# Self-attention followed by a frequency-split convolution: the running maxima spread over other steps, the low parts of kept blocks moved to the end of a step, four of them to GpSimd

## The chip, the cores and the metric

The kernel runs on one core of a Trainium2 chip. Its engines work side by side, each through its own list of instructions, and meet only at semaphores: TensorE (PE; PEld is its weight load), VectorE (DVE), ScalarE (ACT), GpSimd (POOL) and SyncE (SP), which issues all of this kernel's transfers. The metric is the time of one execution on the device, in microseconds (us).

## The reference

Four images of 256 channels and 64 x 64 pixels, all in float32. Layer 0 is self-attention over the 4096 pixels, layer 1 a convolution of two frequency bands:

```python
# layer 0
q = einsum('qc,bcn->bqn', Wq, xf); k = einsum('qc,bcn->bqn', Wk, xf); v = einsum('vc,bcn->bvn', Wv, xf)
attn = softmax(einsum('bqn,bqm->bnm', q, k) * 32 ** -0.5, axis=-1)      # 4096 x 4096 per image
x = gamma[0] * einsum('oc,bchw->bohw', Wo, einsum('bvm,bnm->bvn', v, attn)) + x
# layer 1, on patches of 8 x 8 pixels
low = p.reshape(B * nP, C, 4, 2, 4, 2).mean(axis=(3, 5)); high = p - up2_nearest(low)
low = prelu(bn(einsum('oc,nchw->nohw', mag_w, low) + mag_b))
hs = concatenate([high, roll(high, 1, axis=2)], axis=1)
high = prelu(bn(einsum('oc,nchw->nohw', phase_w, hs) + phase_b))[:, :C]
out = up2_nearest(low) + high
```

## The kernel before

**Turns.** The 4096 query pixels of an image are cut into 8 chunks of 512. One pass over all keys for one chunk is a turn `g`; there are 32 of them. Inside turn `g` three things run interleaved: the attention of chunk `g`, the maxima that the softmax of chunk `g + 1` needs, and the convolution of a chunk whose attention is done. Turns 0 to 23 follow the plan `FULL` (they also project the keys and values of the next image), turns 24 to 30 the plan `LAST`, turn 31 `FINAL`. In turns 0 to 15 (called scan turns here) VectorE also scans a chunk of x of a later image for its largest magnitude (step `SCAN` = 12, L906).

**Steps.** A turn has 32 steps, listed in `UNITS`; each takes one unit, which is 12 matmuls of 128x257 or 128x256 into the four banks `O`. A direct unit `("d", i)` multiplies probabilities that are computed from a product `S` of keys and queries (L597): ScalarE writes them as f16 (`ph`, L765) and as f32 (`p`, L768), VectorE subtracts the two and gives the low part `pl` (L1049). A kept unit `("k", k)` takes scores that were kept in `saved` when their maximum was taken a turn earlier: ScalarE makes `pq` high and the f32 value (L776, L777), VectorE the low part (L1054), and a DMA transposes both into `pt` (L377), because they lie the other way round. Steps 0 to 5 are d0 to d5; then kept and direct units alternate (k0 in step 6, d6 in step 7, k1 in step 8, up to d15 in step 25); steps 26 to 31 are k10 to k15. So in the middle of a turn an even step is a kept unit and an odd step a direct one.

**Tasks.** `Plan` gives each step its tasks. The tasks of a plan take the two banks `M0` and `M1` in turn, so task n can't start on TensorE before task n - 2 has been read out. `("max", j, m)` is one matmul (L526) of 128 queries against 512 keys; VectorE reduces it to a maximum, for m below 4 alone (L949), for m from 4 on it writes the scores to `saved` as well (L953). There are 32 of them in a turn. `steps_with_maxima` gives one to each step from `first` on, and two to the steps in `DOUBLE`. `("negmax",)` turns the maxima into a row for the next turn's products; `("y", h)`, `("low", o)` and `("high", o)` belong to the convolution, `("kq",)` and `("u", h)` to the projections.

**Order on an engine.** The order is written out in the program. In VectorE's step t come first the low part `pl` of the unit of step t + 1, then the low part `pq` of the kept unit of step t + 4, then the scan, then the maxima of step t. SyncE transposes the kept units in their order (`turn_slot`, L374 to L378); between them, at fixed places, it issues the other transfers: after k2 the load `xb` (L422), after k3 the load `xr` that the scan reads (L432), each behind whatever its predecessors wait for. GpSimd splits the frequencies (L301 to L314), makes the low parts of x and of the convolution's input (L1178, L322 to L325), and adds up the output (L1214 to L1223).

Of the kernel before, what the change touches and what calls it, by code (L numbers as in the profile page):

```python
# [29 lines left out]
CH = 512  # L30
# [15 lines left out]

DOUBLE = (7, 8, 10, 12, 14, 16, 18)

ND, NK = MT // 2, MT // 2
# [7 lines left out]
AT = {unit: t for t, unit in enumerate(UNITS)}  # L57
EXP_AHEAD, LOW_AHEAD = 5, 4


def slots_at(t, ahead):

    return [k for k in range(NK) if AT["k", k] - ahead == t]


MAXIMA = [(j, m) for j in range(SUB) for m in range(NCH) if m not in TURNED] + [(j, m) for m in TURNED for j in range(SUB)]


def slot_of(j, m):

    return (m - TURNED[0]) * SUB + j
# [17 lines left out]

def steps_with_maxima(steps, first=4, doubled=DOUBLE):  # L90

    left = list(MAXIMA)
    t = first
    while left:
        for _ in range(2 if t in doubled else 1):
            j, m = left.pop(0)
            assert m not in TURNED or t >= AT["k", slot_of(j, m)] - LOW_AHEAD
            steps.setdefault(t, []).append(("max", j, m))
        t += 1
    steps[t + 1] = [("negmax",)]  # L100
    return steps
# [6 lines left out]
LAST = Plan(steps_with_maxima({4: [("y", 0)], 5: [("y", 1)], 19: [("low", 0, 1)], 21: [("high", 0)], 23: [("high", 1)]},  # L108
                              first=3, doubled=(6, 8, 10, 12, 14, 16, 18)),
            before=(FULL, ALL - NCH))  # L110
# [8 lines left out]
def attention_conv(nc, x, wqk, wv, wo, phase_w, mag_w, params, gamma, alpha, out, q_dram):  # L119
# [7 lines left out]
    with ctx:  # L127
# [103 lines left out]
        s_filled, probs_ready, lo_ready = sem("s_filled"), sem("probs_ready"), sem("lo_ready")  # L231
        slot_probs, slot_low, turn_seen = sem("slot_probs"), sem("slot_low"), sem("turn_seen")
        turned = [sem(f"turned{i}") for i in range(RING)]
        d_weighed, k_weighed, nmax_done, bias_ready = sem("d_weighed"), sem("k_weighed"), sem("nmax_done"), sem("bias_ready")
# [96 lines left out]
        def _(sp):  # L331
# [40 lines left out]
            def turn_slot(g, k):  # L372

                sp.wait_ge(slot_low, NK * g + k + 1)  # L374
                sp.wait_ge(k_weighed, NK * g + k + 1)
# [326 lines left out]
        def _(act):  # L702
# [107 lines left out]
            def turn(g, parity, c, plan, scans):  # L810
# [8 lines left out]
                for t, (unit, i) in enumerate(UNITS):  # L819
                    if t > 0 and unit == "d" and i + LEAD < ND:  # L820
                        probabilities(g, i + LEAD)
                    for k in slots_at(t, EXP_AHEAD):
                        slot_probabilities(g, k)
                    for n, task in plan.numbered.get(t, []):
# [39 lines left out]
        def _(dve):  # L864
# [206 lines left out]
            def take(n, task, g, parity, c, plan):  # L1071
# [12 lines left out]
                elif kind in ("y", "max", "negmax"):  # L1084
# [3 lines left out]
                    elif kind == "max":  # L1088
                        if task[2] in TURNED:
                            dve.wait_ge(slot_low, NK * g + slot_of(*task[1:]) + 1)  # L1090
                            saved_max(bank, task[1], task[2], free)
                        else:
                            partial_max(bank, task[1], task[2], free)
# [11 lines left out]
            def turn(g, parity, c, plan, scans):  # L1105
# [6 lines left out]
                for t in range(MT):  # L1112
                    if t == MT - 2 and plan is LAST:
                        finish_chunk(g)
                    if t + 1 < MT and UNITS[t + 1][0] == "d":
                        low_probabilities(g, UNITS[t + 1][1])
                    for k in slots_at(t, LOW_AHEAD):
                        slot_low_probabilities(g, k)
                    if t == (0 if plan is FULL else 1):
# [6 lines left out]
                    for n, task in plan.numbered.get(t, []):  # L1126
                        take(n, task, g, parity, c, plan)
                    if t == NEGATIVE:
                        negative_parts(plan, g)
# [36 lines left out]
        def _(pool):  # L1166
# [45 lines left out]
            def add_up(g):  # L1212
# [11 lines left out]
                ins.then_inc(out_ready, 1)  # L1224

            def turn(g, parity, c, plan, scans):
                split_frequencies(pool, nc.gpsimd, plan, g)
                if plan is FULL:
                    low_x(0, xbl, xb, xbh, g + EVEN_FIRST + 1)
                low_conv_in(pool, nc.gpsimd, g)  # L1230
                add_up(g)

# [33 lines left out]
```

## Time and profile before

| what | value |
|---|---|
| time, median of 3 runs | 2338.88 us (2338.19 to 2339.94) |
| profiled execution, its own time | 2340.89 us |
| span of the profiled execution | 2338.8 us |
| mean granted TensorE clock | 0.985 |

The span runs from the first to the last instruction; the execution's own time is 2.1 us longer. The turn whose rows are shown below most is turn 12, a scan turn, from 955.8 to 1026.5 us. Its step 9 begins at 976.92, step 13 at 984.81, step 15 at 989.95 and step 17 at 993.55: a direct step begins with its product `S` (L597).

### The profile page before, as it was taken

How to read it: one execution, taken by the hardware profiler on the slowest of the kernel's cores; microseconds unless marked ns; L12 is line 12 of the kernel's file. 1: busy time of each engine (PE TensorE's matmuls, PEld its weight loads, DVE VectorE, ACT ScalarE, POOL GpSimd, SP SyncE). 2: the span in 40 equal slices, each digit the busy share in tenths (PEclk: the TensorE clock that was granted, in tenths of full speed). 3: DMA queues.
4: the chain of work that ended last, by engine and by line, in shares of the span. 5: the costliest groups of instructions: out<-in, count | busy, mean ns of one | idle time of the engine just before them, and what ended most of it. 6: DMA issues, size and time to landing. Idle time of an engine off the chain costs nothing.

```text
span 2338.8 us, 48151 instructions
## 1 busy us (share of the span) xinstructions
PE 2211.5 (95%) x16373; PEld 1768.0 (76%) x16373; DVE 1745.7 (75%) x3388; ACT 1435.3 (61%) x2547; POOL 664.4 (28%) x891
## 2 busy tenths in 40 slices
PE   5799999999989999999998999999999999999997
PEld 4577778777777777777776877777777777777786
DVE  6777787777867777877777777778777777777764
ACT  3456666657656566666575666666666667666664
POOL 3232332232321323322323223223222322333231
PEclk8899999999999999999999999999999999999998
DMA  4255444354654444443565434544446443444443
GB/s 162 62 101 111 103 99 110 72 110 105 146 126 78 103 110 105 99 107 72 112 148 122 99 79 83 110 93 101 99 100 137 87 93 80 81 89 86 84 87 67
DMA packets 596617, 235.02 MB, mean 100 GB/s; under 512 B 547072, under 2 KB 548352, under 8 KB 596576
## 3 DMA queue, kind: packets, MB, share of 16 engines
q1 hardware_dynamic: 596576, 234.51, 46.2%
q8 instruction: 22, 0.36, 0.1%
q14 instruction: 19, 0.16, 0.0%
HBM read 67.67 MB, written 32.53 MB: 43 GB/s over the span
## 4 chain that ended last, share of the span: by engine, by line
PE 74%; ACT 8%; issue 8%; DVE 7%; POOL 1%; DMA 0%; DVEq 0%; SPq 0%; ACTq 0%; POOLq 0%
PE M L489 13%; PE M L526 9%; PE O L651 8%; PE O L653 8%; PE O L652 8%; PE O L638 8%; PE O L640 7%; PE O L639 7%; PE S L597 4%; DVE pmax L949 3%; ACT pq L776 2%; ACT saved L777 2%; ACT p L768 2%; PE M L507 1%; DVE pl L1049 1%
## 5 line engine op out<-in xcount | busy, mean ns | idle before, releaser
L765 ACT ACTIVATE ph<-S 128x512 f16<-128x512 f32 x512 | 308.0, 602 | 540.0 <-PE S L597 537.2
L638 PE MATMUL O<-uh,ph 128*128 128x257 f16 x2048 | 568.7, 278 | 4.4 <-DVE pl L1049 4.0
L651 PE MATMUL O<-uh,pt 128*128 128x257 f16 x2048 | 568.0, 277 | 0.1
L953 DVE TENSOR_SCALAR_CACHE_REDUCE saved<-M 128x512 f32<-128x512 f32 x512 | 346.6, 688 | 292.5 <-PE M L526 287.0
L640 PE MATMUL O<-uh,pl 128*128 128x257 f16 x2048 | 561.9, 274 | 0.0
L639 PE MATMUL O<-ul,ph 128*128 128x256 f16 x2048 | 560.4, 274 | 0.0
L653 PE MATMUL O<-uh,pt 128*128 128x257 f16 x2048 | 558.9, 273 | 0.0
L652 PE MATMUL O<-ul,pt 128*128 128x256 f16 x2048 | 555.6, 271 | 0.0
L526 PE MATMUL M<-kst,qst 96*128 (+1 forms) x1024 | 424.2, 450 | 53.0 <-DVE pmax L949 33.4
L1054 DVE TENSOR_TENSOR pq<-saved,pq 128x512 f16<-128x512 f32 x512 | 379.4, 741 | 86.2 <-ACT saved L777 80.4
L1049 DVE TENSOR_TENSOR pl<-p,ph 128x512 f16<-128x512 f32 x512 | 375.0, 736 | 54.7 <-ACT p L768 53.2
L776 ACT ACTIVATE pq<-saved,nbias 128x512 f16<-128x512 f32 x512 | 369.0, 721 | 0.0
L777 ACT ACTIVATE saved<-saved,nbias 128x512 f32<-128x512 f32 x512 | 368.0, 719 | 0.0
L949 DVE TENSOR_REDUCE pmax<-M 128x1 f32<-128x512 f32 (+1 forms) x512 | 336.5, 683 | 19.6 <-PE M L526 19.4
L768 ACT ACTIVATE p<-S 128x512 f32<-128x512 f32 x512 | 307.6, 601 | 0.0
L638 PEld LDWEIGHTS O<-uh,ph 128*128 128x128 f16 x2048 | 200.4, 98 | 120.2 <-issue 63.5
L651 PEld LDWEIGHTS O<-uh,pt 128*128 128x128 f16 x2048 | 198.8, 97 | 105.2 <-issue 74.3
L526 PEld LDWEIGHTS M<-kst,qst 96*128 96x128 f32 x1024 | 179.5, 191 | 110.9 <-DVE pmax L949 56.3
L1214 POOL TENSOR_TENSOR zlow<-zlow,zlneg 128x256 f32<-128x256 f32 x32 | 35.4, 1106 | 791.0 <-DVE zneg L1069 791.0
L597 PE MATMUL S<-qcur,kst 128*128 128x512 f32 x512 | 237.2, 473 | 18.2 <-ACT p L768 15.8
L640 PEld LDWEIGHTS O<-uh,pl 128*128 128x128 f16 x2048 | 201.2, 98 | 25.7
L653 PEld LDWEIGHTS O<-uh,pt 128*128 128x128 f16 x2048 | 197.7, 97 | 29.1
(161 smaller groups left out, 2864.9 us busy)
## 6 DMA issues: line engine op xcount, KB each, us to landing
xr<-in_x SPq DMA_DIRECT2D x53, 512.0 KB, 3.7
out_y<-z SPq DMA_DIRECT2D x33, 512.0 KB, 3.0
xb<-in_x SPq DMA_DIRECT2D x25, 512.0 KB, 3.9
pt<-pq SPq DMA_TRANSPOSE x512, 3.1
qraw<-q_scratch SPq DMA_DIRECT2D x99, 64.0 KB, 2.0
uh_scratch<-uh_next SPq DMA_DIRECT2D x24, 257.0 KB, 3.1
uh<-uh_scratch SPq DMA_DIRECT2D x24, 257.0 KB, 3.3
ul_scratch<-ul_next SPq DMA_DIRECT2D x24, 256.0 KB, 3.1
```

The lines of the kernel that those rows point to most:

```text
L526: return nc.tensor.matmul(bank[:, :], qst[0:96, j * 128:(j + 1) * 128], kst[0:96, keys_at], start=True, stop=True)
L638: nc.tensor.matmul(O[j][:, 0:UW], ph[:, i % 4, q], uh[:, i, :], start=(i == 0), stop=False)
L639: nc.tensor.matmul(O[j][:, 0:C], ph[:, i % 4, q], ul[:, i, :], start=False, stop=False)
L640: ins = nc.tensor.matmul(O[j][:, 0:UW], pl[:, i % 4, q], uh[:, i, :], start=False, stop=False)
L651: nc.tensor.matmul(O[j][:, 0:UW], pt[:, k % RING, i, :], uh[:, t, :], start=False, stop=False)
L652: nc.tensor.matmul(O[j][:, 0:C], pt[:, k % RING, i, :], ul[:, t, :], start=False, stop=False)
L653: ins = nc.tensor.matmul(O[j][:, 0:UW], pt[:, k % RING, SUB + i, :], uh[:, t, :], start=False, stop=(ends and i == SUB - 1))
L776: nc.scalar.activation(pq[:, k % RING, 0, :], saved[:, k, :], ACT.Exp, scale=SCALE, bias=bias)
L777: nc.scalar.activation(saved[:, k, :], saved[:, k, :], ACT.Exp, scale=SCALE, bias=bias).then_inc(slot_probs, 1)
L949: nc.vector.tensor_reduce(pmax[:, j, ds(m, 1)], bank[:, :], AX.X, ALU.max).then_inc(free, 1)
L1049: nc.vector.tensor_tensor(pl[:, i % 4, :], p32[:, i % 2, :], ph[:, i % 4, :], ALU.subtract).then_inc(lo_ready, 1)
L1054: nc.vector.tensor_tensor(pq[:, k % RING, 1, :], saved[:, k, :], pq[:, k % RING, 0, :], ALU.subtract).then_inc(slot_low, 1)
```

## The change

It has three parts. The maxima begin in step 3 (before: 4 under `FULL`, 3 under `LAST`), the doubled steps are 8, 10, 15, 17, 25 (before: 7, 8, 10, 12, 14, 16, 18), under `LAST` 8, 10, 12, 15, 17, 26, and the `negmax` task comes in the step right behind the last maximum. The low part of a kept unit moves on VectorE from the head of step AT - 4 to the end of step AT - 3 for k0 to k9, behind the maxima of that step, and for k10 to k15 to the end of step AT - 4. And the low parts of k9 to k12 are made by GpSimd, in two halves of 256 columns each, counted by a semaphore of their own.

```diff
-DOUBLE = (7, 8, 10, 12, 14, 16, 18)
+DOUBLE = (8, 10, 15, 17, 25)
...
-EXP_AHEAD, LOW_AHEAD = 5, 4
...
+POOLED = (9, 10, 11, 12)
+EXP_AT = [AT["k", k] - 5 for k in range(NK)]
+LOW_AT = [AT["k", k] - (3 if k < ND - RISE else 4) for k in range(NK)]
...
+def low_count(g, k):
+
+    if k in POOLED:
+        return len(POOLED) * g + POOLED.index(k) + 1
+    return (NK - len(POOLED)) * g + k - sum(p < k for p in POOLED) + 1
...
-def steps_with_maxima(steps, first=4, doubled=DOUBLE):
+def steps_with_maxima(steps, first=3, doubled=DOUBLE):
...
-    steps[t + 1] = [("negmax",)]
+    steps[t] = [("negmax",)]
...
-                              first=3, doubled=(6, 8, 10, 12, 14, 16, 18)),
+                              doubled=(8, 10, 12, 15, 17, 26)),
...
             def turn_slot(g, k):
 
-                sp.wait_ge(slot_low, NK * g + k + 1)
+                sp.wait_ge(pooled_low if k in POOLED else slot_low, low_count(g, k))
+                sp.sem_inc(turn_seen, 1)
                 sp.wait_ge(k_weighed, NK * g + k + 1)
...
-                    for k in slots_at(t, LOW_AHEAD):
-                        slot_low_probabilities(g, k)
...
                     for n, task in plan.numbered.get(t, []):
                         take(n, task, g, parity, c, plan)
+                    for k in range(NK):
+                        if LOW_AT[k] == t and k not in POOLED:
+                            slot_low_probabilities(g, k)
...
+            def pooled_probabilities(g, k):
+
+                pool.wait_ge(slot_probs, NK * g + k + 1)
+                for n in (slice(0, CH // 2), slice(CH // 2, CH)):
+                    ins = nc.gpsimd.tensor_tensor(pq[:, k % RING, 1, n], saved[:, k, n], pq[:, k % RING, 0, n], ALU.subtract)
+                ins.then_inc(pooled_low, 1)
+
...
                 low_conv_in(pool, nc.gpsimd, g)
+                for k in POOLED:
+                    pooled_probabilities(g, k)
                 add_up(g)
```

VectorE, steps 12 and 13 of a scan turn, before. `pl` and `pq` are the low parts of a direct and a kept unit, `amax<-xr` is the scan, each `pmax<-M` a maximum:

```order
L1049 TENSOR_TENSOR pl<-p32,ph 128x512
L1054 TENSOR_TENSOR pq<-saved,pq 128x512
L1124 REGISTER_ALU
L906 ISA
L906 TENSOR_REDUCE amax<-xr 128x1
L1085 REGISTER_ALU
L949 TENSOR_REDUCE pmax<-M0 128x1
L949 TENSOR_REDUCE pmax<-M1 128x1
L1085 REGISTER_ALU
L949 TENSOR_REDUCE pmax<-M0 128x1
```

The same two steps of the changed kernel:

```order
L1056 TENSOR_TENSOR pl<-p32,ph 128x512
L1130 REGISTER_ALU
L913 ISA
L913 TENSOR_REDUCE amax<-xr 128x1
L1092 REGISTER_ALU
L956 TENSOR_REDUCE pmax<-M0 128x1
L956 TENSOR_REDUCE pmax<-M1 128x1
L1061 TENSOR_TENSOR pq<-saved,pq 128x512
```

Between `pl` and the end of step 13 stood `pq`, the scan and three maxima; now the scan and two maxima stand there, and a `pq` (k5, the same unit) behind them.

VectorE, steps 16 and 17, before; `saved,pmax<-M` is a maximum whose scores are kept:

```order
L1049 TENSOR_TENSOR pl<-p32,ph 128x512
L1054 TENSOR_TENSOR pq<-saved,pq 128x512
L1085 REGISTER_ALU
L953 TENSOR_SCALAR saved,pmax<-M0 128x512
L953 TENSOR_SCALAR saved,pmax<-M1 128x512
L1085 REGISTER_ALU
L953 TENSOR_SCALAR saved,pmax<-M0 128x512
```

And in the changed kernel:

```order
L1056 TENSOR_TENSOR pl<-p32,ph 128x512
L1098 ISA
L960 TENSOR_SCALAR saved,pmax<-M1 128x512
L1092 REGISTER_ALU
L1098 REGISTER_ALU
L960 TENSOR_SCALAR saved,pmax<-M0 128x512
L1098 REGISTER_ALU
L960 TENSOR_SCALAR saved,pmax<-M1 128x512
L1061 TENSOR_TENSOR pq<-saved,pq 128x512
```

The number of instructions in the pair is the same; `pq` (k7) moved from the second place to the last, and two of the three maxima now fall into the direct step 17 instead of the kept step 16.

GpSimd, from the last inputs of the convolution to the first row of the output's sum, before:

```order
L322 TENSOR_TENSOR hl<-high,hh 128x256 x4
L324 TENSOR_TENSOR hl<-high,hh 128x2x64
L325 TENSOR_TENSOR ll<-low,lh 128x256
L1214 TENSOR_TENSOR zlow<-zlow,zlneg 128x256
```

And in the changed kernel:

```order
L330 TENSOR_TENSOR ll<-low,lh 128x256
L1237 ISA
L1239 TENSOR_TENSOR pq<-saved,pq 128x256 x2
L1237 REGISTER_ALU
L1239 TENSOR_TENSOR pq<-saved,pq 128x256 x2
L1237 REGISTER_ALU
L1239 TENSOR_TENSOR pq<-saved,pq 128x256 x2
L1237 REGISTER_ALU
L1239 TENSOR_TENSOR pq<-saved,pq 128x256 x2
L1223 TENSOR_TENSOR zlow<-zlow,zlneg 128x256
```

Eight half-size subtractions for k9 to k12 are new there, behind the convolution's inputs and ahead of the output's sum.

## Rows read from the trace of the kernel before

**Rows 1.** Page, part 1: engine, busy us (share of the span), number of instructions.

```profile
PE 2211.5 (95%) x16373; PEld 1768.0 (76%) x16373; DVE 1745.7 (75%) x3388; ACT 1435.3 (61%) x2547; POOL 664.4 (28%) x891
```

**Rows 2.** Waits of the whole span: us in total, times, longest.

```profile
DVE pq L1054 <- ACT saved L777: 80.4, 139, 3.5
PEld M L526 <- DVE pmax L949: 56.3, 81, 1.6
PEld M L526 <- DVE saved L953: 28.2, 39, 2.3
```

**Rows 3.** Timeline of TensorE, steps 9 to 17 of turn 12: start, duration, idle before.

```profile
976.92 0.47 PE L597 MATMUL S<-qcur,kst 128*128 128x512 f32 x1
977.80 0.51 PE L526 MATMUL M<-kst,qst 96*128 x1 [0.41 <-DVE pmax L949]
...
984.81 0.48 PE L597 MATMUL S<-qcur,kst 128*128 128x512 f32 x1
986.53 0.51 PE L526 MATMUL M<-kst,qst 96*128 x1 [1.25 <-DVE pmax L949]
...
989.95 0.47 PE L597 MATMUL S<-qcur,kst 128*128 128x512 f32 x1
990.26 0.39 PE L526 MATMUL M<-kst,qst 96*128 x1
991.74 0.71 PE L526 MATMUL M<-kst,qst 96*128 x2
993.55 0.48 PE L597 MATMUL S<-qcur,kst 128*128 128x512 f32 x1
994.71 0.49 PE L526 MATMUL M<-kst,qst 96*128 x1 [0.68 <-DVE saved L953]
```

**Rows 4.** Line 526 in a turn: what ended its waits; turn 12, then turn 19 (no scan).

```profile
  DVE pmax L949: 3.9, 4
  DVE saved L953: 1.7, 2
...
  DVE saved L953: 1.6, 2
  DVE pmax L949: 1.6, 3
```

**Rows 5.** Timeline of VectorE, steps 12 to 16 of turn 12.

```profile
984.06 0.69 DVE L1054 TENSOR_TENSOR pq<-saved,pq 128x512 f16<-128x512 f32 x1 [0.66 <-ACT saved L777]
984.67 1.21 DVE L906 TENSOR_REDUCE amax<-xr 128x1024 f32 x1
985.80 1.97 DVE L949 TENSOR_REDUCE pmax<-M 128x1 f32<-128x512 f32 x3
...
990.69 0.69 DVE L953 TENSOR_SCALAR_CACHE_REDUCE saved<-M 128x512 f32<-128x512 f32 x1 [0.52 <-PE M L526]
...
992.80 1.25 DVE L1054 TENSOR_TENSOR pq<-saved,pq 128x512 f16<-128x512 f32 x1 [0.30 <-ACT saved L777]
```

**Rows 6.** Page, part 6: transfers, number, size, median us from issue to landing.

```profile
xr<-in_x SPq DMA_DIRECT2D x53, 512.0 KB, 3.7
...
pt<-pq SPq DMA_TRANSPOSE x512, 3.1
```

**Rows 7.** Timeline of SyncE, turn 12: k3's transpose, then the load for the scan.

```profile
977.26 1.25 SPq L377 DMA_TRANSPOSE pt<-pq  x1
978.83 0.40 SPq L432 DMA_DIRECT2D xr<-in_x  x1
```

**Rows 8.** Timeline of GpSimd, turn 12.

```profile
975.60 3.34 POOL L314 TENSOR_TENSOR high<-y,low 128x256 f32<-128x256 f32 x4
980.76 3.24 POOL L1178 TENSOR_TENSOR xbl<-xb,xbh 128x256 fp32r<-128x256 f32 x4 [1.82 <-ACT xbh L843]
989.15 2.79 POOL L322 TENSOR_TENSOR hl<-high,hh 128x256 fp32r<-128x256 f32 x4 [5.16 <-ACT lh L808]
```

**Rows 9.** End of turn 12: TensorE's last maximum and negmax, ScalarE's k12 on the way.

```profile
1009.58 0.71 ACT L777 ACTIVATE saved<-saved,nbias 128x512 f32<-128x512 f32 x1
...
1020.44 0.47 PE L526 MATMUL M<-kst,qst 96*128 x1
1023.42 0.60 PE L532 MATMUL M<-ident,nmax 128*128 128x128 f32 x4
...
1021.91 0.17 DVE L960 TENSOR_SCALAR nmax<-nmax 128x4 f32<-128x4 f32 x1
```

More of the change, by code:

```diff
@@ L57 @@
 AT = {unit: t for t, unit in enumerate(UNITS)}
-EXP_AHEAD, LOW_AHEAD = 5, 4
-def slots_at(t, ahead):
-    return [k for k in range(NK) if AT["k", k] - ahead == t]
+POOLED = (9, 10, 11, 12)
+EXP_AT = [AT["k", k] - 5 for k in range(NK)]
+LOW_AT = [AT["k", k] - (3 if k < ND - RISE else 4) for k in range(NK)]
 MAXIMA = [(j, m) for j in range(SUB) for m in range(NCH) if m not in TURNED] + [(j, m) for m in TURNED for j in range(SUB)]
+def low_count(g, k):
+    if k in POOLED:
+        return len(POOLED) * g + POOLED.index(k) + 1
+    return (NK - len(POOLED)) * g + k - sum(p < k for p in POOLED) + 1
 def slot_of(j, m):
@@ L96, in steps_with_maxima @@
             j, m = left.pop(0)
-            assert m not in TURNED or t >= AT["k", slot_of(j, m)] - LOW_AHEAD
+            assert m not in TURNED or t > LOW_AT[slot_of(j, m)]
             steps.setdefault(t, []).append(("max", j, m))
         t += 1
-    steps[t + 1] = [("negmax",)]
+    steps[t] = [("negmax",)]
     return steps
@@ L232, in attention_conv @@
         slot_probs, slot_low, turn_seen = sem("slot_probs"), sem("slot_low"), sem("turn_seen")
+        pooled_low = sem("pooled_low")
         turned = [sem(f"turned{i}") for i in range(RING)]
@@ L821, in turn @@
                         probabilities(g, i + LEAD)
-                    for k in slots_at(t, EXP_AHEAD):
-                        slot_probabilities(g, k)
+                    for k in range(NK):
+                        if EXP_AT[k] == t:
+                            slot_probabilities(g, k)
                     for n, task in plan.numbered.get(t, []):
@@ L1089, in take @@
                         if task[2] in TURNED:
-                            dve.wait_ge(slot_low, NK * g + slot_of(*task[1:]) + 1)
+                            k = slot_of(*task[1:])
+                            dve.wait_ge(pooled_low if k in POOLED else slot_low, low_count(g, k))
                             saved_max(bank, task[1], task[2], free)
@@ L1127, in turn @@
                         take(n, task, g, parity, c, plan)
+                    for k in range(NK):
+                        if LOW_AT[k] == t and k not in POOLED:
+                            slot_low_probabilities(g, k)
                     if t == NEGATIVE:
```

## The prediction, as it was put on record

> **What bounds the kernel now.** I read the page's first part, then the waits, then the timelines of a turn. TensorE is busy for 2211.5 of 2338.8 us [rows 1]; it sets the end, and what a change can win is the idle time between its matmuls. Of the waits inside the turns most of it belongs to line 526, the products for the maxima: 56.3 + 28.2 = 84.5 us at their weight loads, released by VectorE reading out a bank [rows 2]. VectorE is busy for 1745.7 us only [rows 1], but it is late in places. The timeline shows where. A direct step begins with S, and where nothing waits its maximum follows 0.31 us later (989.95 to 990.26). In step 9 the distance is 0.88, in step 13 it is 1.72, in step 17 1.16 [rows 3]. So 0.57 + 1.41 + 0.85 = 2.83 us are lost in a scan turn. Line 526's waits add up to 5.6 us in turn 12 and to 3.2 us in turn 19, which has no scan [rows 4] (weight load and matmul are both counted, hence more than 2.83); in proportion turn 19 loses 2.83 x 3.2 / 5.6 = 1.6 us.
>
> Why VectorE is late there: back to back it starts an operation of 512 columns every 0.61 us (984.06 to 984.67), and after the scan the next starts 1.13 us on [rows 5]. TensorE takes 993.55 - 989.95 = 3.60 us for an odd and an even step with three maxima [rows 3]. VectorE has five operations for these (`pl`, `pq`, three maxima): 3.05 us, which fits. With the scan it is 4.18 us, 0.6 too much, and in front of that `pq` waited 0.66 us for ScalarE in the head of the step, with the maxima queued behind it [rows 5]. These waits of `pq` sum to 80.4 us [rows 2]. Third, where GpSimd works, `pq` took 1.25 us, not 0.69 [rows 5, 8].
>
> **The change, part by part.**
>
> *Maxima spread.* A second maximum costs TensorE about 0.24 us (0.71 for two, 0.47 for one, [rows 3, 9]) wherever it stands, so the 32 maxima cost the same. What changes is VectorE's load: steps 12 and 13 now hold `pl`, `pq`, the scan and two maxima, 4 x 0.61 + 1.13 = 3.57 us against 3.60 - 0.24 = 3.36 of TensorE. The surplus falls from 0.6 to 0.2 us, and two banks absorb that. The 1.41 us of step 13 go.
>
> *`pq` behind the maxima.* The maxima no longer stand behind a `pq` that waits for ScalarE. What is then late is `pq` itself, and behind it a chain. From the S of an odd step: maximum at +0.31, VectorE takes it up at +0.74 (990.69 against 989.95), `pq` starts at +1.35 and ends at +2.04, about 0.1 for SyncE (my estimate), the transpose lands 3.1 us later: +5.25 [rows 3, 5, 6]. The kept unit is due three steps on. From step 11: 3.36 + 1.79 (989.95 to 991.74 for an odd step) + 0.33 = +5.48. The margin is 0.2 us; before it was a step and a half more. With two maxima in the odd steps (15 to 18) the chain is 0.61 longer and the steps 2 x 0.24 longer: margin 0.1. If `pq` meets GpSimd (1.25 for 0.69), the unit is late by 0.3 to 0.5 us. In turn 12 GpSimd works from 975.6 to 984.0 with a pause and again from 989.15 [rows 8]: k3, k5 or k4, and k6 can be hit.
>
> *What is queued behind.* SyncE takes its list in order. The load `xr` for the scan stands behind k3's transpose and was issued 1.57 us after it (977.26, 978.83) [rows 7]. k3's `pq` now ends at +2.04 of step 9 at the earliest, with GpSimd and TensorE's own wait there nearer +2.8; the transpose is issued at +2.15 to +2.9 where it stood at +0.34 (976.92, 977.26). So `xr` is issued 1.8 to 2.5 us later, at 980.6 to 981.3, and lands 3.7 us on [rows 6]: 984.3 to 985.0. VectorE, relieved of a `pq` and a maximum, would be ready for the scan at about 983.9. It waits 0.4 to 1.1 us, its maxima with it, and TensorE meets that in step 14. I take 0.9 us there, and 0.4 for step 15 or 16, where `pq` k5 follows late. `xb`, behind k2, is later by some 3 us too; ScalarE and GpSimd have room for that, since its product is used a turn later.
>
> *Four low parts on GpSimd.* Its halves cost 0.70 to 0.81 us by the rows of the same shape (2.79 for four, 3.24 for four); f16 operands on GpSimd are in no row, and I bound a half by 0.6 and by 1.25. So k12 is ready at the latest 2.5 us after ScalarE's 1010.29; its product is due at about 1020.8 [rows 8, 9]. On TensorE's path that is nothing: the cover is steps 21 to 24 with the long products of `high`. VectorE saves 4 x 0.61 = 2.4 us in steps 20 to 24, where it isn't waited for: nothing won either.
>
> The Trainium skill, "SBUF — State Buffer", section on the two sides of SBUF, says that VectorE with two SBUF inputs and GpSimd lock one port pair against each other for a whole instruction, and that the loser blocks fully. By that rule eight more GpSimd instructions can hold up VectorE eight times. The 1.25 us of `pq` beside GpSimd's 2.79 agree with it [rows 5, 8]. It changes nothing in the sum if it holds, as the eight fall where VectorE has room.
>
> *negmax.* It follows the last maximum by one step, not two. The last maximum to the ready row takes 1022.08 - 1020.44 = 1.64 us [rows 9]; a step with one maximum is 3.60 - 1.79 - 0.24 = 1.57. So some 0.1 us are new here.
>
> **The sum.** Step 9 keeps part of its wait, because `pl` and `pq` still meet GpSimd's `high`: 0.35 for 0.57. Step 17, with two maxima and a slowed `pl`: 0.3 for 0.85. A scan turn after: 0.35 + 0.9 + 0.4 + 0.3 + 0.1 = 2.05, before 2.83: 0.8 won, 16 x 0.8 = 12.8. I add 0.1 for the maximum that moved from step 5's neighbourhood to the empty step 3: 14.4. Turns 16 to 23 have no scan: 0.35 + 0.7 + 0.1 = 1.15 after (0.7 where `pq` k6 and the doubled step 17 meet GpSimd's `hl`), 1.6 before: 8 x 0.4 = 3.2. Turns 24 to 30 have fewer tasks; I take their loss as two thirds of that, 1.1, by no row, and the gain as half, 7 x 0.2 = 1.4. Together 19 us. From the execution's own 2340.9 this gives 2321.9. The runs shown have their median 2.0 us below the profiled one, so 2320.
>
> **The rivals.**
>
> *A: no new waits.* The chain's 3.1 us and the queue hold, and `xr` comes in time. Then all of 16 x 2.83 + 8 x 1.6 and some 7 x 1.1 is won but the 0.1 of negmax: 45 + 13 + 8 - 3 = 63 us, 2276. For it: the margins are positive on paper, and a unit that is late once gives all later ones room. Against it: `pq` beside GpSimd, and the `xr` load, which can't be early. Halfway, with step 9, 15 and 17 free and only the load late, is 2340.9 - 16 x 1.9 - 8 x 1.2 - 5 - 2 = 2294.
>
> *B: the kept units become the bound (slower).* Each odd step from 7 to 17 waits for its own transpose by the slowed `pq`: places k3 to k6, 0.5 us each, 2.0 in every turn, beside 1.1 for the load, 0.6 in step 17 and 0.35 in step 9. That is 4.05 in a scan turn against 2.83 and 2.95 against 1.6 (or 1.1) elsewhere: 16 x 1.2 + 8 x 1.35 + 7 x 1.8 = 43 slower, 2382. It decides against the change from about 0.8 us of late units in a turn upward. For it: margins of 0.1 to 0.2 us. Against it: a late unit delays the next odd step's S and with it nothing that the next unit's deadline doesn't share, so waits of several units don't add up fully. A mild form gives 2350.
>
> *C: it doesn't do what it says.* The lateness moves from the maxima to the load and the units and the sum is the same, 2334 to 2343.
>
> **How the numbers follow.** Forecast with what lies around it, 2305 to 2334: 0.44. A and halfway: 0.22. C, within 0.2% (4.7 us, about what a measurement of this kernel can tell from no change): 0.13. B: 0.21. Faster is forecast and A, 0.66. The range leaves out A's far end and B's: 2283 to 2352. The forecast's own is 2305 to 2334.
>
> **What would show it.** Right: in the turns' timeline the maximum of step 13 follows S by 0.31 to 0.4; `pq`'s waits for ScalarE (80.4 us) nearly vanish; a new wait of line 906 or of the scan for the transfer `xr`; line 651, which waits for almost nothing now, waits for the transposes; turns without scan gain less than those with it. Wrong: waits of line 651 of over 1 us in a turn, or none at all; a negmax that waits for more than 0.2 us; GpSimd's halves above 1.25 us.

## The result: 0.4% slower, and where the time went

| | time, median (range, runs) | span | granted clock |
|---|---|---|---|
| before | 2340.01 us (2338.19 to 2343.04, 6) | 2338.8 us | 0.985 |
| after | 2349.98 us (2347.21 to 2351.45, 6) | 2347.0 us | 0.985 |

The ratio is 1.0038, 95% interval [1.0027, 1.0048]: 9 us slower, where 19 us were forecast to be won.

Page of the changed kernel, parts 1 and 4 (the second is the chain that ended last, by engine and by line):

```profile
PE 2213.0 (94%) x16373; PEld 1762.8 (75%) x16373; DVE 1685.1 (72%) x3260; ACT 1432.9 (61%) x2547; POOL 859.5 (37%) x1147
...
PE 67%; DVE 11%; issue 8%; DMA 6%; ACT 4%; SPq 2%; POOL 1%; DVEq 0%; ACTq 0%; POOLq 0%
PE M L495 13%; PE M L532 7%; PE O L657 7%; PE O L644 7%; PE O L659 7%; PE O L658 7%; PE O L646 6%; PE O L645 6%; PE S L603 4%; DMA pt<-pq 4%; DVE pq L1061 3%; DMA xr<-in_x 3%; DVE pmax L956 2%; DVE saved L960 2%; PE M L513 1%
```

VectorE has 61 us less to do and GpSimd 195 us more; TensorE's work is the same [rows 1]. The chain now runs through two transfers, the transposes (4%) and the load for the scan (3%); in the kernel before, transfers had 0% of it.

The waits of the whole span (us in total, times, longest), those of [rows 2] and the new ones. Lines are those of the changed kernel: 532 are the maxima, 538 is the product of negmax, 657 the first of a kept unit's matmuls, 913 the scan, 1061 `pq`.

```profile
PEld O L657 <- DMA pt<-pq: 42.0, 95, 2.0
PEld M L532 <- DVE pmax L956: 32.5, 58, 1.4
PEld M L538 <- issue: 29.1, 32, 1.8
DVE amax L913 <- DMA xr<-in_x: 23.4, 15, 2.4
PE M L538 <- DVE nmax L967: 20.7, 32, 1.3
PEld M L532 <- DVE saved L960: 18.6, 25, 2.3
DVE pq L1061 <- ACT saved L783: 17.4, 7, 8.5
```

What the change was to remove went: `pq`'s waits for ScalarE fell from 80.4 to 17.4 us, the maxima's weight loads wait 51.1 us instead of 84.5. Three waits took their place: kept units for their transposes (42.0 us), the scan for its load (23.4 us), and negmax, which waited once in the whole run before and now waits each of its 32 times (24 `FULL` turns, 7 `LAST`, one in the head of the program). These sums aren't time lost one for one: a weight load can wait while matmuls before it still run.

**By turns.** I take a turn from its first product `S` to that of the next and compare the two profiled executions, turn by turn:

| turns | forecast | measured |
|---|---|---|
| 0 to 15, with a scan | -14.4 us | -3.0 us |
| 16 to 23, without | -3.2 us | +6.5 us |
| 24 to 30, `LAST` | -1.4 us | +3.9 us |
| turn 31 and the head of the program | 0 | +0.8 us |
| sum | -19.0 us | +8.1 us (rounded rows: 8.2) |

An ordinary scan turn did get shorter, 70.17 us (turn 12) for 70.67. But turns 16 to 23 went from about 69.0 to 69.85 and `LAST` turns from about 65.0 to 65.7.

**Scan turn 12.** TensorE, steps 9 to 19 (compare [rows 3]; start, duration, idle before):

```profile
974.91 0.48 PE L603 MATMUL S<-qcur,kst 128*128 128x512 f32 x1
...
978.79 0.48 PE L603 MATMUL S<-qcur,kst 128*128 128x512 f32 x1
...
982.35 0.48 PE L603 MATMUL S<-qcur,kst 128*128 128x512 f32 x1
982.67 0.40 PE L532 MATMUL M<-kst,qst 96*128 x1
985.20 0.51 PE L532 MATMUL M<-kst,qst 96*128 x1 [0.79 <-DVE pmax L956]
...
986.80 0.51 PE L603 MATMUL S<-qcur,kst 128*128 128x512 f32 x1
...
990.99 0.48 PE L603 MATMUL S<-qcur,kst 128*128 128x512 f32 x1
...
994.59 0.48 PE L603 MATMUL S<-qcur,kst 128*128 128x512 f32 x1
```

The maximum of step 13 follows its S by 0.32 us (982.35 to 982.67), where it took 1.72 before. The wait has moved one step on: the maximum of step 14 stands 0.79 us for VectorE. Two steps with two maxima take 3.36 us unhindered, with three 3.60. From S to S the pairs beginning with steps 9, 11, 13 and 15 took 3.88, 3.56, 4.45 and 4.19 us (those from 11 and 13 have two maxima, the others three), so they lose 0.28, 0.20, 1.09 and 0.59: 2.16 us together. The pair from step 17 takes its 3.60 and loses nothing.

VectorE and SyncE behind it (compare [rows 5, 7]):

```profile
983.33 1.22 DVE L913 TENSOR_REDUCE amax<-xr 128x1024 f32 x1 [1.36 <-DMA xr<-in_x]
...
977.94 1.24 SPq L383 DMA_TRANSPOSE pt<-pq  x1
979.51 0.40 SPq L438 DMA_DIRECT2D xr<-in_x  x1
```

k3's transpose is issued 3.03 us behind the S of step 9 (0.34 before), the load 1.57 us behind it, and 3.82 us later the scan starts, after a wait of 1.36 us.

**Turn 19, no scan.** TensorE in step 17, VectorE ahead of it, and GpSimd beside it:

```profile
1489.75 0.47 PE L603 MATMUL S<-qcur,kst 128*128 128x512 f32 x1
...
1491.12 0.50 PE L532 MATMUL M<-kst,qst 96*128 x1 [0.67 <-DVE saved L960]
...
1494.28 0.47 PE L603 MATMUL S<-qcur,kst 128*128 128x512 f32 x1
...
1488.10 1.22 DVE L1061 TENSOR_TENSOR pq<-saved,pq 128x512 f16<-128x512 f32 x1
1489.24 1.21 DVE L1056 TENSOR_TENSOR pl<-p,ph 128x512 f16<-128x512 f32 x1
...
1486.66 3.24 POOL L327 TENSOR_TENSOR hl<-high,hh 128x256 fp32r<-128x256 f32 x4 [2.71 <-ACT lh L814]
```

`pq` and `pl` stand one behind the other now and both meet GpSimd's `hl`; each takes 1.2 us for 0.69. The doubled step 17 comes right behind, and from S to S 4.53 us pass for 3.60.

**First turns of an image.** In turn 8 the unit k2 waits, which it did in no turn before:

```profile
697.44 0.28 PE L657 MATMUL O<-uh,pt 128*128 128x257 f16 x1 [1.38 <-DMA pt<-pq]
```

**End of turn 12** (compare [rows 9]): TensorE's last maximum and negmax, VectorE's last row between them, GpSimd's sum of the output.

```profile
1018.73 0.48 PE L532 MATMUL M<-kst,qst 96*128 x1
1021.06 0.62 PE L538 MATMUL M<-ident,nmax 128*128 128x128 f32 x4 [0.50 <-DVE nmax L967]
...
1020.32 0.59 DVE L967 TENSOR_SCALAR nmax<-nmax 128x4 f32<-128x4 f32 x1
...
1017.66 3.23 POOL L1226 TENSOR_TENSOR z<-z,zneg 128x256 f32<-128x256 f32 x4
```

From the last maximum to negmax 2.33 us pass where a step gives 1.57: 0.76 us are lost. And the operation on 128x4 numbers, 0.17 us before, took 0.59 beside GpSimd's `z<-z,zneg`.

**End of turn 26, a `LAST` turn.** The last maximum and negmax again, and VectorE between them:

```profile
1994.02 0.47 PE L532 MATMUL M<-kst,qst 96*128 96x512 f32 x1
1996.89 0.62 PE L538 MATMUL M<-ident,nmax 128*128 128x128 f32 x4 [1.06 <-DVE nmax L967]
...
1994.63 0.83 DVE L1061 TENSOR_TENSOR pq<-saved,pq 128x512 f16<-128x512 f32 x1
1995.49 0.69 DVE L960 TENSOR_SCALAR_CACHE_REDUCE saved<-M 128x512 f32<-128x512 f32 x1
```

Here 2.87 us pass instead of 1.57, so 1.30 are lost in each of these turns. The `pq` of k15, which now stands at the end of step 27, is still in front of the last maximum on VectorE: its product is done at 1994.49 and read from 1995.49 on.

### The profile page after: what moved, and what is told of

The parts are those of the page before. It is cut to its first block, busy times and chain, and to the rows that moved or that the text cites. A ratio compares the mean times of both kernels' runs of the same rounds, so it can differ in the third digit from the quotient of the medians.

```text
span 2347.0 us, 49363 instructions
## 1 busy us (share of the span) xinstructions
PE 2213.0 (94%) x16373; PEld 1762.8 (75%) x16373; DVE 1685.1 (72%) x3260; ACT 1432.9 (61%) x2547; POOL 859.5 (37%) x1147
## 4 chain that ended last, share of the span: by engine, by line
PE 67%; DVE 11%; issue 8%; DMA 6%; ACT 4%; SPq 2%; POOL 1%; DVEq 0%; ACTq 0%; POOLq 0%
PE M L495 13%; PE M L532 7%; PE O L657 7%; PE O L644 7%; PE O L659 7%; PE O L658 7%; PE O L646 6%; PE O L645 6%; PE S L603 4%; DMA pt<-pq 4%; DVE pq L1061 3%; DMA xr<-in_x 3%; DVE pmax L956 2%; DVE saved L960 2%; PE M L513 1%
## 5 line engine op out<-in xcount | busy, mean ns | idle before, releaser
L532 PE MATMUL M<-kst,qst 96*128 (+1 forms) x1024 | 435.1, 447 | 27.0 <-DVE pmax L956 13.7
L1056 DVE TENSOR_TENSOR pl<-p,ph 128x512 f16<-128x512 f32 x512 | 398.6, 780 | 57.9 <-ACT p L774 56.5
L1061 DVE TENSOR_TENSOR pq<-saved,pq 128x512 f16<-128x512 f32 x384 | 297.2, 774 | 17.5 <-ACT saved L783 17.4
L1239 POOL TENSOR_TENSOR pq<-saved,pq 128x256 f16<-128x256 f32 x256 | 181.3, 733 | 330.4 <-ACT saved L783 330.4
L657 PEld LDWEIGHTS O<-uh,pt 128*128 128x128 f16 x2048 | 198.8, 97 | 118.2 <-DMA pt<-pq 42.0
L603 PE MATMUL S<-qcur,kst 128*128 128x512 f32 x512 | 237.8, 475 | 17.7 <-ACT p L774 15.3
L532 PEld LDWEIGHTS M<-kst,qst 96*128 96x128 f32 x1024 | 187.1, 191 | 74.4 <-DVE pmax L956 32.5
L306 POOL TENSOR_TENSOR zneg<-y 128x256 f32<-128x256 f32 x64 | 41.8, 674 | 525.3 <-DVE y L1068 525.3
```

What stands on the lines that cost most here:

```text
L532: return nc.tensor.matmul(bank[:, :], qst[0:96, j * 128:(j + 1) * 128], kst[0:96, keys_at], start=True, stop=True)
L657: nc.tensor.matmul(O[j][:, 0:UW], pt[:, k % RING, i, :], uh[:, t, :], start=False, stop=False)
L1056: nc.vector.tensor_tensor(pl[:, i % 4, :], p32[:, i % 2, :], ph[:, i % 4, :], ALU.subtract).then_inc(lo_ready, 1)
```

## The experiments

Two theories for the loss stood against each other from the start. N: negmax stands too close, and `nmax` is held by GpSimd. K: the kept units' transposes are late, because `pq` stands at the end of a step. Q was a special form of K: the scan's load, queued behind a late transpose, is what costs. Ratios are to the kernel before, with 95% intervals.

| kernel | time (runs) | ratio |
|---|---|---|
| changed, last maximum a step earlier | 2332.62 (5) | 0.9959 [0.9945, 0.9972] |
| changed, GpSimd's sum behind `nmax` | 2342.02 (11) | 1.0000 [0.9991, 1.0010] |
| changed, scan's load first | 2377.21 (4) | 1.0148 [1.0132, 1.0164] |
| changed, low parts a step earlier | 2294.45 (5) | 0.9799 [0.9786, 0.9813] |
| before, with the spread maxima alone | 2323.60 (5) | 0.9913 [0.9900, 0.9927] |
| changed, maxima crowded again, none on GpSimd | 2353.41 (5) | 1.0044 [1.0030, 1.0058] |
| changed, none on GpSimd | 2343.98 (11) | 0.9999 [0.9990, 1.0008] |
| before, with four low parts on GpSimd | 2345.81 (11) | 1.0011 [1.0002, 1.0020] |
| both repairs | 2283.34 (5) | 0.9746 [0.9732, 0.9760] |
| both repairs, none on GpSimd | 2280.29 (5) | 0.9733 [0.9719, 0.9747] |
| low parts earlier, none on GpSimd | 2293.61 (5) | 0.9787 [0.9773, 0.9800] |
| low parts earlier, maxima crowded, none on GpSimd | 2296.83 (5) | 0.9804 [0.9790, 0.9818] |

### negmax two steps behind the last maximum

```diff
-DOUBLE = (8, 10, 15, 17, 25)
+DOUBLE = (8, 10, 15, 17, 25, 26)
...
-    steps[t] = [("negmax",)]
+    steps[t + 1 if doubled is DOUBLE else t] = [("negmax",)]
```

> The changed kernel, but under FULL (turns 0 to 23) step 26 is doubled too, so that the last maximum stands in step 28 and the negmax keeps its step 30, two steps behind; LAST unchanged. Theory N (the negmax that follows its last maximum by one step meets VectorE's small operation on nmax held up by GpSimd, 0.59 us for 0.17, and TensorE waits 0.6 us there in every turn): 24 turns x 0.6 = 14 us less than the changed kernel, 2335 to 2337, and the wait of the negmax row in TensorE's timeline is gone in turns 0 to 23. Rival L (what was lost are the late transposes and the late scan load alone): within 2 us of the changed kernel, 2349, since those are untouched.

Measured: 2332.62 us, 0.0079 below the changed kernel's ratio: 18 us. The waits at line 538 shrank from 32 to 8, those of the turns 24 to 30 and of the head, which the edit leaves alone:

```profile
PEld M L538 <- issue: 11.0, 8, 1.8
PE M L538 <- DVE nmax L967: 8.8, 8, 1.3
```

One step of distance for negmax is worth about 0.75 us in each of the 24 `FULL` turns by the medians, close to the 0.76 at the end of turn 12. Between the two profiled executions it is a little less: from the last `S` of turn 12 to the first of turn 13 24.00 us became 23.35, and the 24 turns together got 15.5 us shorter.

### GpSimd's sum held back until nmax is written

```diff
 def add_up(g, plan):
     pool.wait_ge(zneg_ready, g + 1)
+    if plan is not FINAL:
+        pool.wait_ge(nmax_ready, g + 2)
```

> The changed kernel, but GpSimd begins the output's sum of a turn only after VectorE has finished the operation on nmax (one more semaphore wait on GpSimd). The maxima and the negmax stand where the change put them. If the port between VectorE and GpSimd is the cause (theory N), the operation on nmax takes 0.17 us instead of 0.59, the negmax waits 0.15 us instead of 0.6, and the time falls by 31 x 0.42 = 13 us, to about 2337. If the short distance alone is the cause and GpSimd has no part in it, nothing changes: 2349 to 2351.

Measured: 2342.02 us, 0.0038 less in the ratio, 9 us; forecast were 13, from 31 turns. But in the 7 `LAST` turns the row had taken 0.30 us, not 0.59; 24 x 0.42 is 10. The `nmax` row is back at its old length in every turn (group by line: busy us, mean ns), and in turn 12 negmax follows the last maximum by 1.90 us:

```profile
L967 DVE TENSOR_SCALAR nmax<-nmax 128x4 f32<-128x4 f32 x32 | 5.5, 170 | 1.1
...
1015.70 0.48 PE L532 MATMUL M<-kst,qst 96*128 x1
1017.60 0.62 PE L538 MATMUL M<-ident,nmax 128*128 128x128 f32 x4
```

So the 0.76 us at negmax have two parts: 0.43 come from GpSimd's work beside a 0.17 us operation, 0.33 from the distance. The single instructions in the trace of the changed kernel say how: in all 24 `FULL` turns the operation starts 0.16 us into one of GpSimd's instructions of 0.72 us, and ends 0.03 us after it. The Trainium skill, "SBUF — State Buffer", section on the two sides of SBUF, gives the lock also to a VectorE operation with one input in a two-port mode, held for a whole instruction, and the 0.59 us agree in that the operation is held to the end of GpSimd's. Which mode the operation ran in no row shows.

### The scan's load ahead of k3's transpose

```diff
-                turn_slot(g, 3)
-
                 emptied(sp, plan, g, ("y", 1))
                 if scans:
...
                     sp.dma_start(xr[:, :, :], x_v[ds(g // NCH, 1), ds(g % NCH, 1)]).then_inc(xr_loaded, 16)
+                turn_slot(g, 3)
```

The edit moves the load that stands at this place in the turns without a scan as well.

> The changed kernel, but SyncE issues the load xr ahead of k3's transpose, not behind it. Theory Q (the scan waits for a load that stands behind a transpose which is now late): the 23.4 us that line 906's successor waits for xr vanish, and the maximum of step 14, which is 1.0 us late in a scan turn, is on time. Of this up to 0.4 us come back as waits for k4 and k5, since less room is left for them: 15 turns x 0.6 to 0.9 = 9 to 13 us less, 2337 to 2341. Rival (the late units take its place fully): under 3 us.

Measured: 2377.21 us, 27 slower than the changed kernel. The scan's waits did go (23.4 to 2.7 us), and with them what Q laid to them: in turn 11 the pairs from steps 13 and 15 take 3.38 and 3.59 us, 4.47 and 4.15 in the changed kernel. But the pair from step 11 now takes 5.32 us instead of 3.55 and the one from step 17 4.30 instead of 3.62, and turns 16 to 23, where no scan waits, are 12.8 us longer in all. Q had a cost right and its repair wrong. The turn that shows it most is turn 12: SyncE and TensorE, then the windows (columns: busy us of PE, PEld, DVE, ACT, POOL, then granted clock, DMA share, GB/s):

```profile
985.28 0.45 SPq L428 DMA_DIRECT2D xb<-in_x  x1
986.05 0.39 SPq L436 DMA_DIRECT2D xr<-in_x  x1
987.63 4.37 SPq L383 DMA_TRANSPOSE pt<-pq  x2
...
992.67 0.28 PE L656 MATMUL O<-uh,pt 128*128 128x257 f16 x1 [1.90 <-DMA pt<-pq]
994.78 0.78 PE L602 MATMUL S<-qcur,kst 128*128 128x512 f32 x1
...
990.00:992.00 2.00, 0.78 (x6) 0.43 (x4) 1.96 (x3) 2.00 (x4) 2.00 (x2) 1.00 0.92 117
...
994.00:996.00 2.00, 2.00 (x9) 1.19 (x8) 0.00 (x0) 0.40 (x1) 0.00 (x0) 0.50 0.00 0
```

Both loads, 1 MB, are now in flight when k3's transpose is issued at 987.63, and TensorE can use it only at 992.67, 5.0 us later instead of the 3.1 of [rows 6]; over the 32 turns the median of k3's transpose is 4.7 us here and 3.1 in the changed kernel. TensorE waits 1.90 us, and then it has lost its clock too: granted is 0.50 (the 1.2 GHz level) from 994 to 996, and S takes 0.78 us for 0.48. The clock falls this way in four turns (7, 12, 15, 18); an ordinary scan turn takes 70.9 us, turn 12 72.9. The late load behind the transpose had cost less than an early one in front of it.

### The low parts one step earlier, still behind the maxima

```diff
-LOW_AT = [AT["k", k] - (3 if k < ND - RISE else 4) for k in range(NK)]
+LOW_AT = [AT["k", k] - 4 for k in range(NK)]
```

> The changed kernel, but the low parts of k0 to k9 stand at the end of step AT - 4, one step earlier, still behind the maxima. Theory K (the kept units' transposes are late by the moved low parts): line 657's waits for the transposes, 53.9 us with the weight loads, fall under 5 us, k3's transpose is issued earlier and the scan's load with it: 31 turns x 0.3 to 0.9 us, 2325 to 2340. The low parts would wait for ScalarE again, but behind the maxima, where that costs little. If that wait is what matters, the time stays at 2345 to 2352.

Measured: 2294.45 us, far below the expected 2325 to 2340: 56 us below the changed kernel, 2% below the one before. Waits, then SyncE and VectorE in turn 12:

```profile
DVE amax L913 <- DMA xr<-in_x: 8.3, 14, 1.5
...
PEld O L657 <- DMA pt<-pq: 3.4, 5, 1.8
...
949.46 0.48 PE L603 MATMUL S<-qcur,kst 128*128 128x512 f32 x1
...
950.36 1.24 SPq L383 DMA_TRANSPOSE pt<-pq  x1
951.92 0.40 SPq L438 DMA_DIRECT2D xr<-in_x  x1
...
955.63 1.22 DVE L913 TENSOR_REDUCE amax<-xr 128x1024 f32 x1
```

The transpose of k3 is issued 0.90 us behind the S of step 9 instead of 3.03, in this turn the load lands before the scan asks for it (over the run 8.3 us of its 23.4 are left), and `FULL` turns take 68.1 us for 70.1 (scan) and 69.85 (none), `LAST` turns 64.96 for 65.7. The negmax waits are untouched (29.0 and 20.7 us): K is a loss of its own, and three times that of N. Scan turns get 2.05 us back and turns 16 to 23, where no scan waits, 1.75: the late units alone carry most of it.

### Each part by itself

The spread alone, on the kernel before (`DOUBLE`, `first`, negmax of the change, low parts untouched):

> The kernel before with the maxima's part of the change alone (first step 3, doubled steps 8, 10, 15, 17, 25 and the set of LAST, negmax right behind the last maximum); low parts as before, all on VectorE at the head of step AT - 4. By my prediction's terms the 1.4 us of step 13 go and 0.1 comes for negmax: 16 x 1.2 less, 2320. By theory N the negmax costs 0.4 to 0.6 us in 31 turns, 12 to 19 us, so that 2330 to 2340 comes out.

Measured: 2323.60 us, 20 us faster than before, nearer to the prediction's 2320 than to theory N's 2330 to 2340. The wait of the maxima's weight loads for `pmax` fell from 56.3 to 37.7 us, and negmax came up with 14.2 + 22.5 us (20.7 + 29.1 in the changed kernel), so N costs something without the late units too, but less. All of the gain is in the scan turns (69.1 us for 70.67); turns 16 to 23 stayed nearly as they were (0.9 us less in all), and the seven `LAST` turns, for which the maxima were spread anew as well, took 66.15 us instead of about 65.0.

The late low parts alone, with nothing on GpSimd (the changed kernel with `DOUBLE = (7, 8, 10, 12, 14, 16, 18)`, `first=4` and negmax two steps behind under `FULL`; `LAST` as in the change):

> The changed kernel with the maxima of FULL where they were before (negmax in step 30, two behind the last maximum) and no low part on GpSimd: the later low parts alone; LAST keeps the maxima of the change, whose last one stands in step 28, since the low part of k15 at the end of step 27 allows none earlier. Theory K: waits for the transposes of 0.3 to 0.8 us a turn as in the changed kernel and a late scan load, against maxima that no longer stand behind a waiting low part: 2335 to 2350. If the later low parts were free, 2320.

Measured: 2353.41 us, 10 slower than before and just outside of what I expected. Turns without a scan got shorter (67.6 to 68.2 us for 69.0; turn 16 stayed and turn 23 took 69.3), scan turns longer (71.7 for 70.67). In turn 12 three maxima stand behind the scan in steps 12 and 13, and the scan behind its load:

```profile
995.85 0.58 PE L532 MATMUL M<-kst,qst 96*128 x1 [2.29 <-DVE pmax L956]
...
993.97 1.22 DVE L913 TENSOR_REDUCE amax<-xr 128x1024 f32 x1 [1.32 <-DMA xr<-in_x]
```

Here too a wait of more than 2 us is followed by a granted clock of 0.50 (the 1.2 GHz level, from 996.1 to 999.5 us), which makes it dearer than itself. It happens in ten of the sixteen scan turns, and in sum TensorE spends 31 us more at this level than in the kernel before (mean granted clock 0.978 for 0.985). Up to half of that, 15 us, is the clock's, so this run doesn't weigh the late low parts by themselves; the step from the spread alone (2323.60) to the change without GpSimd's part, at an equal clock, does.

The change without GpSimd's part (`POOLED = ()`):

> The changed kernel with the four low parts back on VectorE (end of step AT - 3 for k9, AT - 4 for k10 to k12). If the four on GpSimd cost nothing and win nothing, as the prediction has it: within 2 us of the changed kernel, 2348 to 2352. If GpSimd's new instructions hold VectorE up: 5 to 10 us less. If they relieve VectorE on the path: more than 2353.

Measured: 2343.98 us. The ratio is 0.0039 lower, 9 us (6 by the medians): it was not free. With all sixteen low parts on VectorE the unit matmuls' weight loads wait 36.9 us for transposes instead of 42.0, and negmax 41.8 instead of 49.8 (both rows of line 538), `nmax` taking 477 ns in the mean for 515. From the last `S` of an ordinary `FULL` turn to the next turn's first 23.88 us pass instead of 24.00, in a `LAST` turn 22.88 instead of 22.98; that is 3.6 us of the whole. Most of the rest lies in the scan turns.

GpSimd's part alone, on the kernel before:

> The kernel before with the low parts of k9 to k12 on GpSimd as the only change (with the one more increment on SyncE that goes with it). Nothing won or lost: 2338 to 2342. If the port costs VectorE time on the path: 2343 or more.

Measured: 2345.81 us, 0.11% slower, about 2.6 us. VectorE's `pq` took 760 ns in the mean for 741; the waits of TensorE stayed as in [rows 2] (57.1 and 28.0 us).

The three edits in a row close the balance: spread -20 us (0.9913), late low parts +20 (to 0.9999), GpSimd +9 (to 1.0038). By turns of the profiled executions the late low parts cost 15.3 us in turns 0 to 15 and 5.9 in turns 16 to 23 and gave 3.7 back in the `LAST` turns; GpSimd's part cost 5.1, 1.5 and 1.1.

### The combinations

Both repairs together (the edits of the first and the fourth experiment):

> The changed kernel with both repairs: every low part one step earlier (as in the run at 2294), and the last maximum of a full turn one step earlier, so that negmax stands two steps behind it. If the late units and the late negmax are two separate losses, the gains of the two runs add: 2294 less the 17 us that the second repair alone brought (2350 to 2333), 2277 us (2273 to 2283), with the wait of negmax on VectorE's nmax from 20.7 us to below 10 and the wait of the unit matmuls for transposes still near 2 us. Rival: they hide each other (a late unit gives nmax its time), then the early low parts alone had already taken it and the time stays at 2290 to 2295.

Measured: 2283.34 us; the step for negmax brings 12 us here (0.9799 to 0.9746) and 18 without the earlier low parts. They add up only in part (2277 was expected for separate losses, 2290 to 2295 if one hid the other); what the second takes from the first isn't shown.

The same without GpSimd:

> The same as the kernel with both repairs, but all sixteen low parts on VectorE. If GpSimd's four blocks cost time only by holding VectorE's 0.17 us nmax behind a GpSimd instruction and by making units late, little of that is left in the full turns: 0 to 3 us below the kernel with both repairs, about 2275. If sharing costs on its own (longer low parts on VectorE while GpSimd works), 6 us or more below it, as the changed kernel lost without the repairs (2350 against 2344). If GpSimd's help is a gain once VectorE is the closer bound, above it.

Measured: 2280.29 us, the fastest of all, 2.7% below the kernel before.

Of the 84.5 us in [rows 2] 10.5 are left (5.1 at `pmax`, 5.4 at `saved`), and the new waits are small. `FULL` turns take 67.4 us, `LAST` turns 64.8.

Low parts earlier and nothing on GpSimd, negmax as in the change:

> The changed kernel with every low part one step earlier and all sixteen on VectorE, negmax one step behind the last maximum as in the change. Theory N (the 0.17 us nmax is held for 0.5 us behind a GpSimd instruction in nearly each turn): z's GpSimd instructions now start earlier in the turn, so nmax falls clear of them in most turns and the time is 2294 less 6 or more, 2280 to 2289 us, nmax's mean below 0.35 us. Rival: the six us of the four low parts were late units alone, which the earlier step has removed: 2292 to 2296.

Measured: 2293.61 us, in the range of the rival. My expectation fell: `nmax` takes 483 ns in the mean of its 32 times, so it is still held in most turns; GpSimd's sum of the output meets it in the same place.

The four low parts on GpSimd thus cost 9 us where kept units were late, and about 3 us in each of the three pairs where they weren't (0.9787 to 0.9799, 0.9733 to 0.9746, 1.0000 to 1.0011; the intervals of the first two pairs overlap). In no pair did they win. In the first of these pairs the 3 us lie at the end of the turns: it is 24.00 us instead of 23.88 from the last `S` of turn 12 to the first of turn 13, and again 22.98 instead of 22.88 in a `LAST` turn. The time goes between the last maximum and negmax; what lengthens it by 0.1 us is not shown.

The order of the low parts without the spread:

> The changed kernel with the low parts one step earlier, none on GpSimd, but the maximum products of a full turn at the steps of the kernel before: the order of the low parts alone, without the spread. The spread alone brought 2343 to 2324, so if it and the order of the low parts are separate, this one stands 15 to 20 us above the kernel with both repairs and nothing on GpSimd: 2290 to 2296. Rival: once no unit is late the crowded maxima cost nothing more, and it is at 2275 to 2283.

Measured: 2296.83 us, 16.5 above the kernel with both repairs and nothing on GpSimd (0.9804 against 0.9733). In these 16.5 us the spread comes with negmax two steps behind. With negmax right behind, as in the 20 us of the spread alone, it is worth 4 us once the low parts stand behind the maxima and early (0.9804 to 0.9787). So the two gains overlap: the order of the low parts by itself is worth more (0.9804, with the maxima of the change under `LAST`) than the spread by itself (0.9913). Against the crowded kernel with late low parts (1.0044) the one step earlier is worth 0.024, 56 us, but some 15 of these are that kernel's clock.

## Why the prediction was wrong

**The bound and the mechanism were right.** TensorE's idle time decided; the maximum of step 13 follows S by 0.32 us (0.31 to 0.4 stated); `pq`'s waits for ScalarE fell from 80.4 to 17.4 us; the scan waits for its load and line 657 for the transposes, which it didn't before. Turn 12's sum of 0.35 + 0.9 + 0.4 + 0.3 = 1.95 us for steps 9 to 17 was measured as 0.28 + 0.20 + 1.09 + 0.59 = 2.16, and moving the low parts forward gives back 2.05 us of a scan turn. The sum agrees in part by luck: the 0.20 are step 11, which I had put at nothing, and step 17, which I had put at 0.3, lost nothing. The loss before was larger than my 2.83, which looked at odd steps alone: from S to S the pairs from steps 9, 13 and 17 took 4.28, 5.14 and 4.56 us, all with three maxima, so 3.18 were lost. One reading was wrong: the `pq` of 1.25 us at 992.80 did not run beside the 2.79 us of [rows 8], which end at 991.94, but beside the `ll` that follows them:

```profile
992.77 0.72 POOL L325 TENSOR_TENSOR ll<-low,lh 128x256 fp32r<-128x256 f32 x1
```

**The step that failed: negmax, "some 0.1 us are new here".** It is 0.76 us. I took the time to the ready row (1.64) from before, where the row was not held, and ended it there: with the row unheld TensorE's product follows the last maximum by 1.90 us, so 0.33 comes from the distance alone. And I did not ask what GpSimd does in that step, although I had written down that `pq` beside it takes 1.25 us. GpSimd's sum ran there before as well, but the operation that it held was the next one, `nbias` (L962, 591 ns in the mean), for which TensorE doesn't wait:

```profile
1020.58 2.78 POOL L1217 TENSOR_TENSOR z<-z,zneg 128x256 f32<-128x256 f32 x4
...
1022.11 0.59 DVE L962 TENSOR_SCALAR nbias<-nmax 128x4 f32<-128x4 f32 x1
```

So GpSimd is not new at this place; what changed is the moment. Before, `nmax` started 0.64 us into one of GpSimd's instructions, 0.08 from its end, and took the 0.17 us of [rows 9]; now it starts 0.16 into one and takes 0.59. Over 24 turns the term is 24 x 0.66 = 16 us more than I put in, and the experiments give 18 (without other repairs) and 12 (with them). Under `LAST`, where I put in nothing for it, negmax comes 1.30 us late, 9 us over 7 turns; this is read from the rows and was not tested. Together that is about 25 of the 27 us between the forecast -19.0 and the measured +8.1; the terms below miss both ways.

**`LAST` turns: "I take their loss as two thirds of that, 1.1, by no row".** The loss was there and was larger. In turn 27 of the kernel before, the pairs from steps 9, 13 and 17 took 4.28, 3.98 and 4.01 us, all with three maxima, so 1.47 were lost. In the changed kernel the first two lose nothing and the third 0.68 (4.28 us), and with the earlier low parts that goes as well (3.63), 0.75 us a turn. But the late negmax takes 1.30 back. So these turns, about 65.0 us before, take 65.7 in the changed kernel and still 64.8 in the best one, and the forecast gain of 1.4 us became a loss of 3.9.

**Turns without a scan: 0.35 + 0.7.** The late units cost 1.75 us there (69.85 to 68.1), not 1.05. I had named the place, step 17 beside GpSimd's `hl`, but costed one slow operation; `pq` and `pl` are both slow, 0.93 us in turn 19. Step 9 lost 0.32 there (3.92 us to the next S), and the pairs from steps 11 and 13, which I had put at nothing, 0.15 and 0.47 (3.51 and 3.83 for 3.36).

**First turns of an image.** I treated them like the others. k2 waits 1.4 us for its transpose in turn 8; together with negmax turns 8 and 16 are 1.0 and 1.7 us longer than before.

**GpSimd's four low parts, "nothing".** 3 us by themselves, 9 in this kernel. The halves took 0.73 us, inside my bounds of 0.6 and 1.25, and k9 to k12 themselves were never late: in ordinary turns their matmuls begin at the unhindered distance, as I had expected. The difference shows in waits elsewhere, at line 657 and at negmax (about 0.1 us a turn, 3.6 in all); how the four blocks bring them about I did not settle.

**What came of the rivals.** The number is that of the mild form of B (2350). From about 0.8 us of late units a turn on, B said, the change loses, and it was 2.05 and 1.75. But with negmax repaired under `FULL` the change wins in spite of them (2332.62), and no rival had a late negmax: that the number agrees is in part luck. The gain that A saw was there as well (its 63 us are what the best kernel has, 2343.1 to 2280.3, though by turns it is 49, 13 and 2 us where A had 45, 13 and 8, less 3), but only with each low part one step earlier and negmax two steps behind the last maximum in the `FULL` turns. The margin that I had worked out for the kept units, 0.1 to 0.2 us, was the warning: with operations that take 0.69 or 1.22 us depending on GpSimd, it is no margin. The sum should have carried it as a loss.

**What stays open.** negmax still waits in turns 24 to 30 of the best kernel (with the head 8 times, 8.0 us at line 538), and nothing was tried there. Of the 9 us of GpSimd's part in this kernel some 5 have no operation to them.

## What to carry to other kernels

An operation that feeds a transfer has two dates, its own and that of everything queued behind the transfer. Taking it out of the way of the maxima was right and worth 1.3% (0.9913 to 0.9787); taking it one step later at the same time cost 2.1% (0.9787 to 0.9999). So move it within its step first, count the margin to its user with the slow duration of every operation in the chain, and treat a margin smaller than the difference between slow and fast as a wait. And when a short operation on the critical path is moved, look at what GpSimd does at its new place, and count it as held to the end of a GpSimd instruction: length is no protection, and that it ran free before may be a matter of 0.1 us.

## What the chip showed beyond that

- A VectorE operation on 128x4 numbers, f32, from one tile to itself, takes 0.17 us with GpSimd held back (mean of 32). Beside GpSimd's `z<-z,zneg` (0.72 us each) it depends on the moment: begun 0.64 us into such an instruction 0.17 us, begun 0.44 into it 0.30, begun 0.16 into it 0.59 (24, 7 and 24 turns). In the last two cases it ended 0.03 us after GpSimd's instruction.
- A transpose of SBUF tiles that lands 3.1 us after its issue took 5.0 us with 1 MB of loads issued 2.4 and 1.6 us ahead of it (the DMA share was still 0.92 in the window 990 to 992); the median of 32 such turns is 4.7 us.
- After TensorE had waited for 1.90 us, and in another kernel for 2.29, its granted clock fell from 1.00 to 0.50, in the first from 993.0 to 996.4 us, in the second from 996.1 to 999.5. In the second kernel this came in ten of sixteen scan turns and cost up to 15 us.
